# Layer order and rounding in a four-layer image kernel: the previous image's projection moved behind the next image's layer 1, scores set between its chunks, x transposed from the token tile, conv1's high part rounded by ScalarE

## The chip, the cores and the metric

The kernel runs on one core of a Trainium2 chip. The time is that of one launch on the device, in microseconds (us). Three runs of the kernel before gave 1370.06 us at the median, from 1369.67 to 1373.99. The engines are TensorE (PE in the profile, PEld its weight loads), VectorE (DVE), ScalarE (ACT), GpSimd (POOL) and SyncE (SP), which issues every DMA of this kernel.

## What is computed

The input x is 8 images of 64 x 64 pixels with 48 channels, float32. Four layers run one after the other on each image. Biases and norms are left out here; the kernel folds them into its weights.

```python
# L0: attention over the 4096 pixels n of an image, then three convolutions
q2 = l2n(q*q / sum_c(q*q), axis=channel);  k2 = l2n(k*k / sum_c(k*k), axis=pixel)
t2 = q2 @ (k2^T @ v) / sqrt(N);  attn = (v + t2) @ w_ln
y = leaky_relu(conv1x1(concat(attn, x), w1), 0.2)      # "conv1", 96 -> 96
y = leaky_relu(conv3x3(y, w2), 0.2)                    # "conv2", 96 -> 96
x = conv1x1(y, w3) + x                                 # "w3",    96 -> 48
# L1 and L3: relu, depthwise 3x3, pointwise 48 -> 48, norm
# L2: rw = sigmoid(mean(x) @ Wr) mixes 4 experts' weights for this image;
#     expand 48 -> 192, relu, depthwise 3x3, relu, project 192 -> 48, + x
```

## The kernel before, in words

**One loop over images, two images in it.** Each engine has its own hand-written instruction order. `iteration(f, attn, back)` works on three images: it runs conv2, w3, layer 1 and the routing and expansion of layer 2 for image `f`; the rest of layer 2 (depthwise taps, projection), layer 3 and the output of image `back` = f-1; and the attention and conv1 of image `attn` = f+1. Iterations 1 to 6 are a loop; iteration 0 has no `back`, iteration 7 no `attn`. A prologue does attention and conv1 of image 0, and an epilogue layers 2 and 3 of image 7. Engines meet only through semaphores.

**Chunks.** Conv1 and conv2 work in 8 chunks (512 pixels each, one PSUM bank), the layers on row pairs in 4. PSUM is four rings of two banks: a chunk may be written when the reader of the chunk two places before is done.

**Float32 as two parts.** The inputs of conv2, layer 1 and layer 3 are split into a rounded high part and a low part (the difference), and each convolution is three passes: high weights on high input, low weights on high input, high weights on low input. For conv1's output y1 and chunk k: ScalarE writes 0.2 times the bank into a buffer of `y1` (three buffers), VectorE takes the maximum with the bank (`L666`), VectorE rounds it into `y1_h` (`L668`), and GpSimd writes the low part `y1_l` (`L954`). `conv2` waits ahead of its first pass for all 8 high parts and ahead of its third for all 8 low parts.

**Pair convolutions (layers 1 and 3).** `pair_conv` needs neighbour rows in other partitions. `copy_beside` copies them from SBUF to SBUF with 7 DMAs for each half of the image (`L849`, `L853`). The first half can be copied when high and low parts of chunks 0 to 2 are there, the second when chunk 3 is. Chunks 0 and 1 of the convolution wait for the first half, chunks 2 and 3 for the second. Afterwards `copy_x2` (`L862`, 4 DMAs) copies layer 1's output for the expansion of layer 2.

**Layer 2 on VectorE.** The depthwise taps are 50 steps for an image on VectorE (`L623`, `L627`; the first tap of units 2 to 5 is ScalarE's). `steps_at` deals them out: 4 beside conv1, 40 beside conv2, 6 beside the projection. ScalarE's `finish_unit` does the relu of a finished unit, of which `project` chunk m needs numbers up to m + 2. `project` m writes a bank; ScalarE's `project_affine` turns it into layer 3's input `v` and its high part (`L1340`, `L1341`), and VectorE's `l3_low_part` makes the low part (`L704`). `project` m + 2 needs the high part of m.

**Order before, middle iterations.** TensorE: conv2 with w3(m) behind each odd pair, project 0, w3(3), project 1, layer 1 chunks 0 and 1, project 2 and 3, x transposes 0 and 1 (`L1006`), layer 1 chunk 2, transposes 2 and 3, layer 1 chunk 3, all scores (`L1018`), routing (`L1107`), layer 3 (4 chunks), attention sums (`L1030`), output transposes (`L1176`), attention weights, expansion and conv1 of the next image. SyncE: copies for layer 1, load of x in columns into the tile of the depthwise output (`load_xa`, 8 DMAs), copies for layer 3, load of x into the token tile (`load_x`, 8 DMAs), `copy_x2`, store.

## Time and profile before

| what | us |
|---|---|
| median of three runs | 1370.06 |
| profiled execution, its own time | 1369.96 |
| its span, from first to last instruction | 1368.2 |
| TensorE busy in it | 1211.5 (89%) |
| VectorE busy | 906.6 (66%) |
| ScalarE busy | 475.9 (35%) |
| GpSimd busy | 218.2 (16%) |

The span is 1.8 us short of the execution's own time. The six middle iterations repeat every 157.0 us to within a tenth, so one of them is read in detail: from the moment image 4's conv2 waits for its low parts to the same moment of image 5 (694.96 to 851.93). Idle time of TensorE is what to look for first, then what each engine was waiting for; a digit in the row PEclk of the page, or "PEclk" in a table of stretches, is the granted clock as a share of 2.4 GHz, and 0.50 is 1.2 GHz.

### The profile page before, as it was taken

To read this page: it belongs to the slowest core of one execution; us is meant where nothing else is said; L and a number is where in the kernel's file an instruction comes from. 1 tells how busy PE (TensorE), PEld (TensorE's weight loads), DVE (VectorE), ACT (ScalarE), POOL (GpSimd) and SP (SyncE) were. 2 spreads that over 40 slices of the span, in tenths; PEclk is the share of its full clock that TensorE was granted. 3 is DMA by queue.
4 is the path that set the end of the run, shared out by engine and by line. 5 is a ranking of instruction groups with operands and counts; after the bars stand their busy time and mean duration, and the time that the engine had idled before them with its cause. 6 is when DMAs were issued, how large, how long until landed. Compare 5 with 4: busy or idle time off the path is not lost.

```text
span 1368.2 us, 14700 instructions
## 1 busy us (share of the span) xinstructions
PE 1211.5 (89%) x4981; PEld 779.2 (57%) x4981; DVE 906.6 (66%) x1146; ACT 475.9 (35%) x812; POOL 218.2 (16%) x80
## 2 busy tenths in 40 slices
PE   3798788999789996999789996999879997999995
PEld 3565565657455674656556573656656574555543
DVE  5642477954978368964789358983789449884660
ACT  2211431335422542335512444235413354224331
POOL 0300034000610026000430007000340006000000
PEclk9699877999899997999989997999979998999998
DMA  3203700099003960079101980049300990039306
GB/s 59 42 14 43 105 0 0 1 127 123 23 0 39 135 97 0 0 93 135 43 0 25 121 126 0 0 66 139 66 0 0 128 120 23 0 40 127 60 11 91
DMA packets 200076, 76.06 MB, mean 56 GB/s; under 512 B 191245, under 2 KB 191858, under 8 KB 200050
## 3 DMA queue, kind: packets, MB, share of 16 engines
q1 hardware_dynamic: 200050, 75.73, 39.7%
q8 instruction: 15, 0.25, 0.1%
q14 instruction: 11, 0.09, 0.0%
HBM read 13.65 MB, written 6.29 MB: 15 GB/s over the span
## 4 chain that ended last, share of the span: by engine, by line
PE 50%; issue 18%; POOL 15%; SPq 7%; DVE 4%; DMA 3%; ACT 2%; POOLq 0%; DVEq 0%; ACTq 0%
PE bank L1074 29%; POOL y_parts L954 13%; PE bank L1098 4%; PE bank L1085 3%; SPq L828 3%; PE bank L1018 2%; SPq L853 2%; PE bank L1142 2%; PE bank L1165 2%; PE bank L1164 2%; POOL tok L949 2%; DMA y_parts<-a_parts 2%; PE bank L1101 1%; PE bank L1100 1%; SPq L849 1%
## 5 line engine op out<-in xcount | busy, mean ns | idle before, releaser
L1074 PE MATMUL bank<-y_parts,w_h 96*96 96x512 f32 x1152 | 329.9, 440 | 49.8 <-POOL y_parts L954 28.2
L1074 PEld LDWEIGHTS bank<-y_parts,w_h 96*96 96x96 f32 x1152 | 202.1, 177 | 162.8 <-POOL y_parts L954 31.6
L627 DVE SCALAR_TENSOR_TENSOR dwa<-h1a,dyn,dwa 128x1024 f32<-128x1024 f32 x240 | 294.1, 1273 | 0.0
L954 POOL TENSOR_TENSOR y_parts<-y,y_parts 96x512 fp32r<-96x512 f32 x64 | 194.8, 3044 | 211.7 <-DVE y_parts L668 211.7
L627 DVE SCALAR_TENSOR_TENSOR dwb<-h1b,dyn,dwb 128x1024 f32<-128x1024 f32 x128 | 155.8, 1273 | 0.0
L1074 PE MATMUL bank<-y_parts,w_l 96*96 96x512 f32 x576 | 153.9, 413 | 0.0
L949 POOL TENSOR_TENSOR tok<-tok,u 128x1536 f32<-128x1536 f32 x8 | 22.4, 2797 | 735.7 <-DVE u L568 735.7
L1098 PE MATMUL bank<-a_parts,wt_h 128*96 128x512 f32 x384 | 119.2, 419 | 15.9 <-DMA y_parts<-a_parts 15.9
L1074 PEld LDWEIGHTS bank<-y_parts,w_l 96*96 96x96 f32 x576 | 98.0, 170 | 47.5 <-issue 0.6
L1313 ACT ACTIVATE xq<-bank,b2s 96x512 f32<-96x512 f32 x32 | 21.9, 685 | 236.2 <-PE bank L1074 227.3
L704 DVE SCALAR_TENSOR_TENSOR a_parts<-v,a_parts 96x512 fp32r<-96x512 f32 x64 | 44.0, 687 | 85.8 <-ACT a_parts L1341 83.0
L1059 PE MATMUL bank<-xq,w_cur 97*96 97x512 f32 x128 | 70.0, 628 | 29.2 <-DVE y L666 28.5
L668 DVE CAST y_parts<-y 96x512 fp32r<-96x512 f32 x64 | 90.0, 1407 | 2.2
L1098 PEld LDWEIGHTS bank<-a_parts,wt_h 128*96 128x96 f32 x384 | 61.5, 165 | 46.8 <-issue 20.8
L1313 ACT ACTIVATE y<-bank,b2s 96x512 f32<-96x512 f32 x32 | 21.9, 684 | 144.1 <-PE bank L1074 144.1
L1030 PE MATMUL bank<-tok 128*97 128x48 f32 x512 | 55.0, 277 | 16.7 <-POOL tok L949 16.7
L681 DVE SCALAR_TENSOR_TENSOR xq<-bank,col,xq 96x512 f32<-96x512 f32 x32 | 23.8, 744 | 64.8 <-ACT xq L1313 64.8
L1164 PE MATMUL bank<-dwa,pc 128*96 128x512 f32 x128 | 65.4, 592 | 0.0
L1165 PE MATMUL bank<-dwb,pc 128*96 128x512 f32 x128 | 65.3, 592 | 0.0
L1030 PEld LDWEIGHTS bank<-tok 128*97 128x97 f32 x512 | 54.9, 195 | 17.9 <-issue 17.0
L717 DVE TENSOR_TENSOR y_parts<-y,y_parts 96x512 fp32r<-96x512 f32 x32 | 22.1, 689 | 60.6 <-ACT y_parts L1354 60.6
L1098 PE MATMUL bank<-a_parts,wt_l 128*96 128x512 f32 x192 | 57.4, 408 | 0.0
(222 smaller groups left out, 1700.1 us busy)
## 6 DMA issues: line engine op xcount, KB each, us to landing
y_parts<-a_parts SPq DMA_DIRECT2D x32, 396.0 KB, 6.1
y_parts<-a_parts SPq DMA_DIRECT2D x64, 192.0 KB, 6.6
a_parts<-a_parts SPq DMA_DIRECT2D x32, 264.0 KB, 3.3
dwa<-in_x_dram SPq DMA_DIRECT2D x64, 96.0 KB, 2.9
tok<-in_x_dram SPq DMA_DIRECT2D x64, 96.0 KB, 4.2
x_even<-y_parts SPq DMA_DIRECT2D x16, 384.0 KB, 8.8
x_odd<-y_parts SPq DMA_DIRECT2D x16, 384.0 KB, 8.6
out_dram<-dwb SPq DMA_DIRECT2D x32, 192.0 KB, 2.2
```

The lines of the kernel that those rows point to most:

```text
L627: nc.vector.scalar_tensor_tensor(out=dst, in0=tap_input(n, t), scalar=weight, in1=dst, op0=ALU.mult, op1=ALU.add).then_inc(tap_step, 1)
L668: nc.vector.tensor_copy(y1_view(y1_h, k - 1), y1_tokens(k - 1)).then_inc(y1h_ready, 1)
L704: return nc.vector.scalar_tensor_tensor(out=lo[:, rows, 1:W + 1], in0=src[:, m % 2, :].rearrange("p (j w) -> p j w", w=W), scalar=0.0, in1 ...
L949: nc.gpsimd.tensor_tensor(k, k, columns(u[:, :, :], 2 * RUN, [[1, 2 * RUN], [0, C]]), ALU.mult).then_inc(k_scaled, 1)
L954: nc.gpsimd.tensor_tensor(y1_view(y1_l, k), y1_tokens(k), y1_view(y1_h, k).bitcast(F32), ALU.subtract).then_inc(y1l_ready, 1)
L1030: last = nc.tensor.matmul(bank[0:SUMS, 0:C], token(par, i, X_AT, SUMS), token(par, i, K_AT, C), start=first, stop=final)
L1059: nc.tensor.matmul(bank[0:C2, :], w1_cur[:, :], xq[:, (k - 1) % 2, :], start=True, stop=True)\
L1074: last = nc.tensor.matmul(bank[0:C2, :], wgt[:, t, :], src[:, rows, cols], start=t + n == 0, stop=t == TAPS - 1 and n == 2)
L1098: nc.tensor.matmul(bank[0:C2, :], wgt[layer][:, kw, :], own[:, rows, kw:kw + W], start=n + kw == 0, stop=False)
L1164: nc.tensor.matmul(bank[0:C2, :], pc[:, 0, cols], first[:, :, par, :], start=False, stop=False)
L1165: last = nc.tensor.matmul(bank[0:C2, :], pc[:, 1 + m // 2, cols], other[:, :, par, :], start=False, stop=par == 1)
L1313: nc.scalar.activation(y2[(k // 2) % 2][:, (k % 2) * BANK:(k % 2 + 1) * BANK], ring_c.bank(C_2 + k)[0:C2, :], ACT.Identity, bias=b2s[:, 0: ...
```

## The change

Six things are changed.

1. **Projection.** `project`, `project_affine` and the copies for layer 3 of image `back` move from beside layer 1 of image `f` to behind it: project 0, routing, project 1 to 3, attention sums, layer 3 chunks 0 and 1, attention weights, chunks 2 and 3. On VectorE, `norms_begin` (the norms of the attention) now stands ahead of `route`, and `norms_end` between `l3_low_part` 1 and 2.
2. **Scores and transposes.** x transposes 0 and 1 come ahead of w3(3), 2 and 3 behind layer 1 chunk 0; scores 0 to 3 behind chunk 1 and 4 to 7 behind chunk 2.
3. **x from the token tile.** `load_xa` is gone. `load_x` is first in SyncE's iteration and has 12 DMAs: x, and the even rows once more beside the odd ones in the place of q, so that `transpose_x` reads pairs from the token tile.
4. **Conv1's rounding.** ScalarE copies the bank unscaled (`y1_linear`), VectorE forms max(0.2 y, y) from SBUF alone in one instruction, ScalarE rounds to the high part (`y1_high_part`), GpSimd writes the low parts of chunks 0 to 6 and VectorE that of chunk 7 (`y1l_last`).
5. **Conv2.** w3(m) goes behind the first pass of chunk 2m + 2, where it was behind all three; the wait for low parts stays ahead of the third pass of chunk 0.
6. **Taps.** 6 beside conv1, 4 beside each conv2 chunk, 12 beside layer 1. q's fourth powers go to `y1`, layer 1's output buffer to `xq`.

```diff
-        steps_at = (0, 1, 1, 1, 0, 1, 0, 0) + (8, 5, 5, 5, 5, 4, 4, 4) + (1, 1, 1, 3)
+        steps_at = (0, 1, 1, 1, 1, 1, 1, 0) + (4,) * CHUNKS + (1, 1, 2, 3, 3, 2)
-        expand_beside = {BEFORE: (0, 1), 0: (2,), 1: (3, 4), 7: (), 8: (10, 11), **{k: (k + 3,) for k in range(2, 7)}}
+        expand_beside = {BEFORE: (0, 1), 7: (), 8: (9, 10, 11), **{k: (k + 2,) for k in range(7)}}
 # VectorE, conv1_out
-                    dve.wait_ge(y1_slope, CHUNKS * image + k)
-                    bank = ring_c.bank(C_1 + k - 1)
-                    nc.vector.tensor_tensor(y1[:, buffer, :], bank[0:C2, :], y1[:, buffer, :], ALU.max).then_inc(y1_max, 1)
-                    dve.wait_ge(y1_max, CHUNKS * image + k)
-                    nc.vector.tensor_copy(y1_view(y1_h, k - 1), y1_tokens(k - 1)).then_inc(y1h_ready, 1)
+                    dve.wait_ge(y1_linear, CHUNKS * image + k)
+                    nc.vector.scalar_tensor_tensor(out=y1[0:C2, buffer, :], in0=y1[0:C2, buffer, :], scalar=SLOPE,
+                                                   in1=y1[0:C2, buffer, :], op0=ALU.mult, op1=ALU.max).then_inc(y1_max, 1)
+                if image is not None:
+                    dve.wait_ge(y1h_ready, CHUNKS * image + CHUNKS)
+                    nc.vector.tensor_tensor(y1_view(y1_l, CHUNKS - 1), y1_tokens(CHUNKS - 1),
+                                            y1_view(y1_h, CHUNKS - 1).bitcast(F32), ALU.subtract).then_inc(y1l_last, 1)
 # VectorE, iteration: behind the last x2_low_part
-                route(f)
-                if attn is not None:
-                    norms_begin(attn)
-                mix_weights(f)
-                if attn is not None:
-                    norms_end(attn)
+                depthwise_at(back, BY_L1 + 5)
+                if attn is not None:
+                    norms_begin(attn)
+                route(f)
+                for m in range(2) if back is not None else ():
+                    l3_low_part(back, m)
+                if attn is not None:
+                    norms_end(attn)
+                for m in range(2, PCHUNKS) if back is not None else ():
+                    l3_low_part(back, m)
+                mix_weights(f)
 # ScalarE, iteration: behind l1_out(f, (3,))
+                if attn is not None:
+                    fourth_powers(attn)
                 if back is not None:
                     project_affine(back, f + 1, 0)
                     finish_unit(back, 4)
                     finish_unit(back, 5)
                 route(f)
-                if attn is not None:
-                    fourth_powers(attn)
+                for m in range(1, PCHUNKS) if back is not None else ():
+                    project_affine(back, f + 1, m)
+                if attn is not None:
+                    root_of_q(attn)
                 if back is not None:
                     l3_out(back, (0, 1))
 # SyncE
             def iteration(f, attn, back):
+                if attn is not None:
+                    load_x(sp, attn)
                 beside_l1(sp, f)
-                if attn is not None and back is not None:
-                    load_xa(sp, attn, PCHUNKS * (f - 1) + 2)
                 if back is not None:
                     beside_l3(sp, back, f + 1)
-                if attn is not None:
-                    load_x(sp, attn)
                 copy_x2(sp, f)
 # GpSimd
-                for k in range(CHUNKS):
+                for k in range(POOL_CHUNKS):      # 7
```

**TensorE, from the end of layer 1 to layer 3 of a middle iteration.** Before (L1101 is layer 1 and 3, L1018 scores, L1107 routing, L1030 sums, L1176 output):

```order
L1101 MATMUL bank<-y_parts,wt_h 96x512
...
L1018 MATMUL bank<-qkw,xcm 128x192 x2
...
L1107 MATMUL bank<-wr,mean_b 128x4
...
L1098 MATMUL bank<-a_parts,wt_h 96x512 x3
...
L1030 MATMUL bank<-tok 97x48 x32
L1176 MATMUL bank<-ident,dwa 128x96 x16
```

Now (L1087 is layer 1, L1149 to L1151 the projection, L1093 routing, L1014 sums, L1084 layer 3):

```order
L1087 MATMUL bank<-y_parts,wt_h 96x512
...
L1149 MATMUL bank<-x_even,pick 96x512
L1150 MATMUL bank<-dwa,pc 96x512
L1151 MATMUL bank<-dwb,pc 96x512
...
L1093 MATMUL bank<-wr,mean_b 128x4
...
L1149 MATMUL bank<-x_even,pick 96x512
...
L1014 MATMUL bank<-tok 97x48 x32
...
L1084 MATMUL bank<-a_parts,wt_h 96x512 x3
```

Between the last chunk of layer 1 and the first of layer 3 stood the scores and the routing; now the four chunks of the projection stand there, then the sums.

**VectorE, the same place.** Before (L717 is `x2_low_part`, L729 `route`, L566 to L574 `norms_begin`, L741 the start of `mix_weights`, L581 and L584 `norms_end`):

```order
L717 TENSOR_TENSOR y_parts<-y,y_parts 96x8x64 [waits x2h_ready]
L729 TENSOR_TENSOR rwz<-bank,br 128x4 [waits rw_done]
...
L566 TENSOR_REDUCE s<-tok 128x64 [waits squared]
...
L574 TENSOR_SCALAR s<-s 128x64 [waits attn_chain]
L741 TENSOR_TENSOR prod<-lin,rw 128x92 [waits rw_ready]
...
L581 RECIPROCAL r<-s 128x32 [waits root_q]
...
L584 TENSOR_TENSOR tok<-tok,r 128x32x48 [waits attn2_chain]
```

Now (L629 a tap, L568 to L576 `norms_begin`, L731 `route`, L706 `l3_low_part`, L583 and L586 `norms_end`):

```order
L719 TENSOR_TENSOR y_parts<-xq,y_parts 96x8x64 [waits x2h_ready]
...
L629 SCALAR_TENSOR_TENSOR dwa<-h1a,dyn,dwa 128x1024 [waits tap_step]
...
L568 TENSOR_REDUCE s<-tok 128x64 [waits squared]
...
L731 TENSOR_TENSOR rwz<-bank,br 128x4 [waits rw_done]
L706 SCALAR_TENSOR_TENSOR a_parts<-v,a_parts 96x8x64 [waits ah3_ready,v3_ready] x2
L583 RECIPROCAL r<-s 128x32 [waits root_q]
...
L586 TENSOR_TENSOR tok<-tok,r 128x32x48 [waits attn2_chain]
L706 SCALAR_TENSOR_TENSOR a_parts<-v,a_parts 96x8x64 [waits ah3_ready,v3_ready] x2
L743 TENSOR_TENSOR prod<-lin,rw 128x92 [waits rw_ready]
```

`norms_begin` passed ahead of `route`, and the low parts of layer 3's chunks 2 and 3 stand behind the whole of the norms.

**ScalarE, the same place**, now (L1256 fourth powers, L1344 and L1345 `project_affine`, L1363 `route`, L1260 `root_of_q`); before, all of `project_affine` stood ahead of the end of layer 1:

```order
L1256 ACTIVATE y<-tok 128x1536 [waits squared]
...
L1344 ACTIVATE v<-bank,dyn 96x512 [waits al1_ready]
L1345 ACTIVATE a_parts<-bank,dyn 96x8x64
...
L1363 ACT_TABLE_LOAD
L1363 ACTIVATE rw<-rwz 128x4 [waits rwz_ready]
...
L1344 ACTIVATE v<-bank,dyn 96x512 [waits al1_ready,project_done]
...
L1344 ACTIVATE v<-bank,dyn 96x512 [waits al3_ready,project_done]
...
L1260 ACT_TABLE_LOAD
L1260 ACTIVATE s<-s 128x32 [waits norm_q]
```

`project_affine` 1 to 3 stand behind `route`, and `root_of_q` behind them.

## Rows read from the trace of the kernel before

**Rows 1.** The page: busy us of each engine (share of the span), instructions.
```profile
PE 1211.5 (89%) x4981; PEld 779.2 (57%) x4981; DVE 906.6 (66%) x1146; ACT 475.9 (35%) x812; POOL 218.2 (16%) x80
```

**Rows 2.** Table of stretches, one middle iteration: length, each engine's busy us, clock, DMA.
```profile
core 0: us, PE busy (x) PEld busy (x) DVE busy (x) ACT busy (x) POOL busy (x), PEclk, DMA share, GB/s
694.96:749.50 54.54, 54.54 (x211) 35.45 (x212) 48.07 (x45) 12.88 (x16) 0.00 (x0) 0.96 0.04 7
749.50:784.30 34.80, 33.45 (x122) 18.44 (x121) 14.46 (x17) 14.91 (x25) 0.00 (x0) 1.00 1.02 128
784.30:813.50 29.20, 28.32 (x179) 22.54 (x177) 15.88 (x34) 14.81 (x32) 2.80 (x1) 1.00 0.96 127
813.50:851.93 38.43, 27.36 (x106) 16.66 (x103) 33.45 (x37) 16.64 (x28) 25.91 (x8) 0.84 0.05 20
```

**Rows 3.** Timeline of TensorE, conv2 starts: start us, us, instructions [idle before <-releaser].
```profile
683.85 4.16 PE L1074 MATMUL bank<-y_parts,w_h 96*96 96x512 f32 x9 [3.17 <-DVE y_parts L668]
...
694.96 6.55 PE L1074 MATMUL bank<-y_parts,w_h 96*96 96x512 f32 x18 [4.18 <-POOL y_parts L954]
...
703.49 4.47 PE L1074 MATMUL bank<-y_parts,w_h 96*96 96x512 f32 x18
```

**Rows 4.** Timeline of GpSimd, low parts of y1, chunks 6 and 7.
```profile
838.61 1.69 POOL L954 TENSOR_TENSOR y_parts<-y,y_parts 96x512 fp32r<-96x512 f32 x1 [0.55 <-DVE y_parts L668]
840.85 11.03 POOL L954 TENSOR_TENSOR y_parts<-y,y_parts 96x512 fp32r<-96x512 f32 x1 [0.55 <-DVE y_parts L668]
```

**Rows 5.** Timeline of VectorE beside them: maximum, rounding, eight taps.
```profile
838.46 0.67 DVE L666 TENSOR_TENSOR y<-bank,y 96x512 f32<-96x512 f32 x1
839.17 1.60 DVE L668 CAST y_parts<-y 96x512 fp32r<-96x512 f32 x1
840.69 9.64 DVE L627 SCALAR_TENSOR_TENSOR dwb<-h1b,dyn,dwb 128x1024 f32<-128x1024 f32 x8
```

**Rows 6.** Timeline of TensorE from projection 1 to the output transposes.
```profile
754.59 0.79 PE L1163 MATMUL bank<-x_even,pick 96*96 96x512 f32 x1
...
758.49 1.28 PE L1098 MATMUL bank<-a_parts,wt_h 128*96 128x512 f32 x3
...
784.23 1.46 PE L1018 MATMUL bank<-qkw,xcm 97*128 97x192 f32 x8
...
791.11 0.93 PE L1098 MATMUL bank<-a_parts,wt_h 128*96 128x512 f32 x3
...
805.45 5.61 PE L1030 MATMUL bank<-tok 128*97 128x48 f32 x64
810.89 2.35 PE L1176 MATMUL bank<-ident,dwa 96*128 96x96 f32 x16
```

**Rows 7.** Timeline of VectorE: last low part of layer 1's output, norms.
```profile
785.99 0.69 DVE L717 TENSOR_TENSOR y_parts<-y,y_parts 96x512 fp32r<-96x512 f32 x1 [0.20 <-ACT y_parts L1354]
...
791.76 3.35 DVE L566 TENSOR_REDUCE s<-tok 128x64 f32<-128x3072 f32 x1 [0.30 <-ACT tok L1260]
...
799.11 0.18 DVE L574 TENSOR_SCALAR s<-s 128x32 f32<-128x32 f32 x1
...
805.13 1.76 DVE L584 TENSOR_TENSOR tok<-tok,r 128x1536 f32<-128x1536 f32 x1
```

**Rows 8.** Timeline of ScalarE: the second half of project_affine 0, a table load.
```profile
754.16 0.68 ACT L1341 ACTIVATE a_parts<-bank,dyn 96x512 fp32r<-96x512 f32 x1
...
791.74 1.28 ACT L1359 ACT_TABLE_LOAD   x1
```

**Rows 9.** Timeline of SyncE: first DMA of layer 3's first-half copies, iteration 4.
```profile
773.82 0.65 SPq L849 DMA_DIRECT2D a_parts<-a_parts  x1
```

**Rows 10.** Epilogue: SyncE issues the same copies, TensorE waits; a stretch of the DMA.
```profile
1330.91 0.65 SPq L849 DMA_DIRECT2D a_parts<-a_parts  x1
...
1342.81 1.57 PE L1098 MATMUL bank<-a_parts,wt_h 128*96 128x512 f32 x3 [10.17 <-DMA y_parts<-a_parts]
...
1350.00:1352.00 2.00, 2.00 (x10) 1.39 (x9) 0.00 (x0) 0.00 (x0) 0.00 (x0) 1.00 0.36 32
```

More of the change, by code:

```diff
@@ L819, in x_rows @@
             return a["x"][image].rearrange("(j b) (q i) c -> b q j i c", b=2, q=WQ)
-        def load_xa(sp, image, projected):
-            src = x_rows(image)
-            wait(sp, project_done, projected)
-            by_column = xa.rearrange("p (i b c) -> p b i c", b=2, c=C)
-            for n in range(2 * WQ):
-                par, q = n % 2, n // 2
-                sp.dma_start(by_column[q::WQ, par], src[par, q]).then_inc(xa_loaded, 16)
         def load_x(sp, image):
@@ L836, in load_x @@
                 sp.dma_start(tok[q::WQ, par, :, X_AT:X_AT + C], src[par, q]).then_inc(x_loaded, 16)
+            for q in range(WQ):
+                sp.dma_start(tok[q::WQ, 1, :, Q_AT:Q_AT + C], src[0, q]).then_inc(x_loaded, 16)
         def copy_beside(sp, n, half):
@@ L1180, in l1, with l3, prepare_norms @@
                 pair_conv(image, L1, ring_b, B_L1, l1_done, chunks)
-            def l3(image):
-                pair_conv(image, L3, ring_d, D_L3, l3_done, range(PCHUNKS))
+            def l3(image, chunks):
+                pair_conv(image, L3, ring_d, D_L3, l3_done, chunks)
+            def prepare_norms():
+                pe.wait_ge(prep_dve, marks["pairs"])
+                pe.wait_ge(wt_placed, 16 * WT_COPIES)
+                nc.tensor.matmul(banks[7][:, 128:128 + C], ones[0:C, :], norm3[:, :], start=True, stop=True).then_inc(prep_pe, 1)
+                for n in range(2):
+                    rows, cols = slice(0, (M1, M2)[n]), slice(n * M1, (M1, M)[n])
+                    nc.tensor.matmul(banks[7][0:C2, 192 + cols.start:192 + cols.stop], ones[rows, 0:C2], norm1[rows, cols],
+                                     start=True, stop=True).then_inc(prep_pe, 1)
@@ L1187, in iteration @@
+                if attn is not None:
+                    attention_scores(attn, range(4, 8))
+                l1(f, (3,))
                 if back is not None:
                     project(back, (0,))
-                w3(f, PCHUNKS - 1)
-                if back is not None:
-                    project(back, (1,))
-                else:
-                    pe.wait_ge(prep_dve, marks["pairs"])
-                    pe.wait_ge(wt_placed, 16 * WT_COPIES)
-                    nc.tensor.matmul(banks[7][:, 128:128 + C], ones[0:C, :], norm3[:, :], start=True, stop=True).then_inc(prep_pe, 1)
-                    for n in range(2):
-                        rows, cols = slice(0, (M1, M2)[n]), slice(n * M1, (M1, M)[n])
-                        nc.tensor.matmul(banks[7][0:C2, 192 + cols.start:192 + cols.stop], ones[rows, 0:C2], norm1[rows, cols],
-                                         start=True, stop=True).then_inc(prep_pe, 1)
@@ L1251, in x_out, with scores_out @@
                         .then_inc(xcm_ready, 1)
-            def scores_out(image):
-                for n in range(8):
+            def scores_out(image, banks_of_two):
+                for n in banks_of_two:
                     act.wait_ge(qk_done, 8 * image + n + 1)
@@ L1409, in iteration @@
                 if back is not None:
-                    l3_out(back, (0, 1))
+                    project_affine(back, f + 1, 0)
+                    finish_unit(back, 4)
+                    finish_unit(back, 5)
+                route(f)
+                for m in range(1, PCHUNKS) if back is not None else ():
+                    project_affine(back, f + 1, m)
                 if attn is not None:
```

178 lines of the change are left out of this document (87 added, 91 removed).

## The prediction

> **What bounds the kernel now.** I read the page's busy shares first: TensorE is busy 89% of the span, no other engine over 66% [rows 1]. So the question is where TensorE idles and whether the change fills those holes or makes new ones. The table of stretches answers it for one middle iteration of 157.0 us [rows 2]: TensorE idles 0.0, 1.3 and 0.9 us in the first three stretches and 11.1 us in the last, conv1 of the next image and the start of conv2. There the clock is 0.84 on average; elsewhere it is full or nearly. The timeline shows the end of that stretch: conv2 waits 3.2 us for VectorE's last high part, and behind 18 matmuls 4.2 us for GpSimd's last low part [rows 3]. A second reading of rows 2 matters more here: from 749.5 to 813.5 the DMA share is 1.02 and 0.96, the copies run all through layers 1 and 3, and yet TensorE hardly waits for them. Layer 3's first copies are issued at 773.82 [rows 9], and layer 3 starts at 791.11 [rows 6], 17.3 us later; the projection was done early enough. That cover is what the change takes away.
>
> **Conv1 and the start of conv2.** GpSimd and VectorE exclude each other here: the last low part takes 11.03 us where the one before takes 1.69 [rows 4], because eight taps of 9.64 us run from 840.69 [rows 5] and it finishes about 1.6 us after them. The rounding of 1.60 us ends 0.5 us after the low part beside it, but the maximum of 0.67 us, with one input in PSUM, costs GpSimd nothing [rows 4, 5]. The change makes chunk 7's low part VectorE's and ahead of the taps, so the 4.2 us wait goes. What is late next is the chain of exclusive work before it. Before: 7 low parts of 1.69 (11.8 us), 8 roundings of about 0.6 (5), 4 taps (4). Now: 7 low parts (11.8), 8 maxima that read SBUF twice, of 0.65 (5.2), 6 taps (6.4), and one more turn to ScalarE and back. ScalarE has four instructions a chunk of 0.59 on average (16.64 us for 28 in that stretch [rows 2]), 2.4 us, beside it. I take conv2 starting 1 us later than now; at best the rest of the stretch's idle time goes (11.1 - 4.2 = 6.9 us), at worst it starts 5 us later, if each turn to ScalarE costs 0.6 us. Conv2's start now also loses about 5 us at half clock: 9 matmuls take 4.16, later 18 take 4.47 [rows 3]. Without the second stop I estimate 4 lost. Sum: -4.2 + 1 - 1 = -4.2 us.
>
> [...]
>
> **From conv2's end to layer 1's end.** This takes 34.9 us now (749.4 to 784.2), with the projection's 4 x 3.9 us in it (754.59 to 758.49 is one) [rows 6]. Now the scores (6.9 us, 784.23 to 791.11) take its place. w3 comes 18 matmuls (4.4 us [rows 3]) earlier: w3(2) ends 45 matmuls, 10.7 us, ahead of conv2's end. The sum with the shortcut, the high part, two taps and the low part take about 4.4 (1.1, 0.6, 2.4, 0.7; estimates but for the taps), and the first half of the copies is issued at -6.1. How long a half takes stands in the epilogue: 1330.91 to 1342.81, 11.9 us [rows 10]. Layer 1 could start at +3.3 (my estimate: the last y2 on two engines 1.5, w3 1.7) and starts at +5.8. Its four chunks take 3.6 us each (791.11 to 805.45 is four) [rows 6]. Adding transposes (0.9), two groups of scores (3.8 each) and a low clock at its start (1), layer 1 ends at +29.7. The second half, issued at +6.6, lands at +18.5, when TensorE gets there. Sum: 29.7 - 34.9 = -5.2 us. Between -8 and 0, by the wait for the copies. The x loads go to conv2, where the DMA share is 0.04 [rows 2]: they cost nothing, and the 1.3 us of idle in the second stretch, the transposes' wait for them, goes.
>
> **From layer 1's end (t = 0, now 784.23) to the expansion (now 813.5, +29.3).** Step by step:
> - VectorE ends layer 1's last low part at +2.4 (785.99 + 0.69) [rows 7], two taps of 1.2 at +4.8, `norms_begin` (791.76 to 799.29, 7.5 us) at +12.3. Only then `route`, +12.5. The routing's wait thus has the norms queued ahead of it.
> - ScalarE finishes project_affine 0 and two units at +7.4, loads its table (1.28) [rows 8] and stands at `route` until +12.7. project_affine 1 is two instructions of 0.68, +14.0.
> - TensorE runs projection 0 to 2 by +11.9; number 3 needs the high part of 1 and runs from +14.1 to +18.0. Idle 2.2.
> - project_affine 3 at +19.4; table load and root at +20.9; `norms_end` (the 1.76 of rows 7 and two short ones, 2.3) at +23.3; only then VectorE's low part 2 at +24.0. SyncE issues layer 3's first half at +24.3. It lands 11.9 later, **+36.2**.
> - TensorE ends the sums (5.4) [rows 6] at +23.5 and idles **12.7 us**. After such a stop layer 3's first chunk ran 6.0 us in the epilogue (from 1342.81, at 0.50 clock), so chunks 0 and 1 end at +45.8. Both halves land 19.7 us after the first issue (in 1350 to 1352 the share falls to 0.36) [rows 10], +44.0: no further wait.
> - Chunks 2 and 3 with the weights 7.6, outputs 2.35 behind a wait of 1: **+56.7**. `copy_x2` is behind these copies on SyncE and lands near +55.3 to +59: about level.
> Sum: 56.7 - 29.3 = +27.4 us. Least +22 (no low clock, a shorter norm chain), most +31.
>
> **The sum.** A middle iteration: -4.2 - 5.2 + 27.4 = +18.0, six times +108. The last iteration has no norms; its low part 2 comes at about +14, its half at +26 against sums that do not exist: about 10.4 idle, 2.4 at low clock, and the layer 1 wait, +17. Iteration 0 has no projection: conv1 -4, and copies and scores moved ahead about -3, -7. The prologue loads 12 where 8 DMAs came before the first transposes (+2.5) and has one low part less (-2). Total +118 or +119 on the execution's 1369.96 (span 1368.2, 0.1 below the median): **1489 us**.
>
> **The rivals.**
> A. Conv1 is no longer held by the exclusive pair: the new maximum or ScalarE's share lets conv1 run at TensorE's own pace, 5 to 8 us less per image, seven times: 1489 - 45 = 1444. For: VectorE loses eight roundings of up to 1.60. Against: two SBUF inputs, as the taps have, and two taps more. Chance 0.09.
> B. The turn VectorE, ScalarE, GpSimd with three buffers sets the pace: +4 us per image, or copy_x2 lands at +59: 1489 + 31 = 1520. For: ScalarE must now answer twice per chunk. Chance 0.17.
> C. The other side: layer 3 does not wait for its copies. Place: between the sums and layer 3. If the first half lands by +23.5, where the sums end, the 12.7 idle and 2.4 of low clock go, and with the 2.2 ahead of projection 3 the iteration is 157.7, within a us of now; the last one is +5, iteration 0 -7: 1372, and with A's gain 1330. It decides at the issue: SyncE would have to start at +11.6 and not at +24.3. For: now it starts 17 us ahead. Against: three waits in a row (route behind the norms, projection 3, norms_end) stand before it. Chance 0.05, half of it faster, and 0.01 of it slower.
> D. The chain is shorter than I add it up, because ScalarE or VectorE gets ahead: half of the 12.7 us is there, 1489 - 45: again 1444. Chance 0.09.
>
> **How the numbers follow.** The forecast has 0.60, A and D 0.18, B 0.17, C 0.05. The range holds all but C and the ends of A and B: 1438 to 1530. A measurement of this kernel can tell about 0.3% (4 us) from no change. Slower: 0.96; same: 0.015; faster: 0.025.
>
> **What would show it.** TensorE's longest wait of a middle iteration should be ahead of layer 3's chunk 0, released by a DMA into y_parts, 10 to 14 us, with the clock at 0.50 behind it; a second one of 2 to 3 us ahead of layer 1. The period should be about 175 us. GpSimd's 11 us low part should be gone, and with it the 4.2 us of rows 3. DMA share should be near zero in the 20 us ahead of layer 3's copies. I am wrong if layer 3's copies are issued less than 18 us after layer 1's end, or if the last stretch of rows 2, from the expansion to conv2's third pass (38.4 us), comes out below 32 or over 39.

## The result, and the profile after

The changed kernel took 1492.6, 1489.15 and 1486.73 us, the kernel before 1370.27 us at the median of four runs beside them: a ratio of 1.0864, 95% interval 1.0828 to 1.09. A fourth run of the changed kernel fell in a slow state (2025.76 us at a clock of 0.55) and is compared with nothing. The prediction was 1489 us. Below, a difference from the changed kernel is counted from 1489.15 us, the median of the three. The profiled execution took 1492.6 us, with a span of 1490.8.

The page of the changed kernel, busy us of each engine (compare [rows 1]):

```profile
PE 1241.5 (83%) x4981; PEld 789.0 (53%) x4981; DVE 871.8 (58%) x1090; ACT 531.8 (36%) x876; POOL 170.3 (11%) x72
```

TensorE has the same 4981 matmuls and is busy 30.0 us longer, at a lower mean clock (0.903, before 0.928); the other 92.6 us of the 122.6 that the span grew are idle time. The table of stretches of image 4's iteration has the boundaries of [rows 2]: conv2's third pass, its end, the end of layer 1, the expansion, the next third pass. The columns are length, busy us of TensorE, its weight loads, VectorE, ScalarE and GpSimd, clock, DMA share and GB/s:

```profile
747.76:800.05 52.29, 52.29 (x212) 33.91 (x211) 43.87 (x41) 12.78 (x16) 0.00 (x0) 1.00 0.09 16
800.05:829.46 29.41, 24.11 (x113) 17.11 (x112) 16.46 (x17) 11.69 (x31) 0.00 (x0) 1.00 0.56 62
829.46:887.07 57.61, 42.76 (x187) 25.89 (x186) 21.18 (x43) 16.97 (x26) 2.79 (x1) 0.85 0.64 74
887.07:921.42 34.35, 27.50 (x104) 16.52 (x104) 26.03 (x25) 24.60 (x36) 19.01 (x7) 0.90 0.24 57
```

Against [rows 2] the four are -2.2, -5.4, **+28.4** and -4.1 us. Three stretches gained, and the third lost more than twice what they gained. The middle iterations are not all alike: from third pass to third pass they take 173.1 to 177.0 us, 174.6 on average, and those of the kernel before 157.0 to 157.7 us, 157.3 on average (not 157.0 to within a tenth). TensorE's timeline shows its waits there (start, us, instructions, idle before and releaser). Layer 1's end is 829.46, where projection 0 starts:

```profile
843.37 0.46 PE L1149 MATMUL bank<-x_even,pick 96*96 96x512 f32 x1 [1.84 <-ACT a_parts L1345]
...
845.32 1.42 PE L1149 MATMUL bank<-x_odd,pick 96*96 96x512 f32 x1
...
849.02 5.61 PE L1014 MATMUL bank<-tok 128*97 128x48 f32 x64
...
866.55 1.60 PE L1084 MATMUL bank<-a_parts,wt_h 128*96 128x512 f32 x3 [11.91 <-DMA y_parts<-a_parts]
...
884.92 2.37 PE L1162 MATMUL bank<-ident,dwa 96*128 96x96 f32 x16 [0.96 <-ACT dwa L1368]
```

The 11.91 us are the longest wait of the iteration. What held the copies stands in VectorE's timeline:

```profile
834.23 3.34 DVE L568 TENSOR_REDUCE s<-tok 128x64 f32<-128x3072 f32 x1
...
841.66 0.15 DVE L731 TENSOR_TENSOR rwz<-bank,br 128x4 f32<-128x4 f32 x1
841.73 0.68 DVE L706 SCALAR_TENSOR_TENSOR a_parts<-v,a_parts 96x512 fp32r<-96x512 f32 x1
843.35 0.69 DVE L706 SCALAR_TENSOR_TENSOR a_parts<-v,a_parts 96x512 fp32r<-96x512 f32 x1 [0.94 <-ACT a_parts L1345]
852.05 0.35 DVE L583 RECIPROCAL r<-s 128x32 f32<-128x32 f32 x1 [8.01 <-ACT s L1260]
...
854.34 1.29 DVE L706 SCALAR_TENSOR_TENSOR a_parts<-v,a_parts 96x512 fp32r<-96x512 f32 x2
```

`route` (L731) stands behind 7.4 us of `norms_begin`. VectorE then idles 8.01 us for ScalarE's root with the low parts of chunks 2 and 3 queued behind that wait, though the high part of chunk 2 had been there since 844.4. SyncE's timeline has the issue right behind the first of them, and the table of stretches shows the 20 us ahead of it, the wait, and layer 3's first chunk:

```profile
855.13 0.59 SPq L841 DMA_DIRECT2D a_parts<-a_parts  x1
```

```profile
835.10:855.10 20.00, 17.69 (x91) 10.11 (x89) 10.71 (x15) 8.30 (x12) 2.79 (x1) 0.91 0.00 0
854.64:866.55 11.91, 0.00 (x1) 0.01 (x1) 6.01 (x22) 0.00 (x0) 0.00 (x0) 0.65 1.03 137
866.55:872.60 6.05, 6.05 (x16) 4.03 (x17) 0.00 (x0) 0.00 (x0) 0.00 (x0) 0.55 1.20 139
```

For 20 us no DMA runs while TensorE works, then for 11.9 us TensorE stands while all DMA engines work. Of the two stops of [rows 3] at conv2's start, the 4.18 us are gone and the 3.17 us are 0.78; ahead of the last chunk of conv1 stands a stop of 3.29 us, before 2.33:

```profile
909.40 1.94 PE L1043 MATMUL bank<-xq,w_cur 97*96 97x512 f32 x2 [3.29 <-ACT xq L1275]
...
915.54 3.56 PE L1060 MATMUL bank<-y_parts,w_h 96*96 96x512 f32 x9 [0.78 <-ACT y_parts L1296]
918.90 2.68 PE L1060 MATMUL bank<-y_parts,w_l 96*96 96x512 f32 x9
921.42 4.43 PE L1060 MATMUL bank<-y_parts,w_h 96*96 96x512 f32 x18
```

In conv1 the long low part of [rows 4] is gone, and GpSimd's rows read like this (all 56 of them took 2649 ns on average, before 3044):

```profile
898.81 17.09 POOL L939 TENSOR_TENSOR y_parts<-y,y_parts 96x512 fp32r<-96x512 f32 x6 [0.59 <-ACT y_parts L1296]
```

### The profile page after: what moved, and what is told of

Its sections match the earlier page's. It is cut to its first block, busy times and chain, and to the rows that moved or that the text cites. A ratio compares the mean times of both kernels' runs of the same rounds, so it can differ in the third digit from the quotient of the medians.

```text
span 1490.8 us, 14638 instructions
## 1 busy us (share of the span) xinstructions
PE 1241.5 (83%) x4981; PEld 789.0 (53%) x4981; DVE 871.8 (58%) x1090; ACT 531.8 (36%) x876; POOL 170.3 (11%) x72
## 4 chain that ended last, share of the span: by engine, by line
PE 44%; issue 32%; POOL 8%; DMA 5%; SPq 5%; ACT 3%; DVE 3%; POOLq 0%; ACTq 0%; DVEq 0%
PE bank L1060 29%; POOL y_parts L939 6%; DMA y_parts<-a_parts 5%; PE bank L1071 4%; PE bank L1084 3%; SPq L845 2%; PE bank L1128 2%; SPq L841 2%; POOL tok L934 1%; PE bank L1003 1%; DVE y L667 1%; PE bank L1086 1%; PE bank L1087 1%; ACT y_parts L1296 1%; PE bank L1014 1%
## 5 line engine op out<-in xcount | busy, mean ns | idle before, releaser
L1060 PE MATMUL bank<-y_parts,w_h 96*96 96x512 f32 x1152 | 300.0, 414 | 2.8 <-ACT y_parts L1296 2.8
L629 DVE SCALAR_TENSOR_TENSOR dwa<-h1a,dyn,dwa 128x1024 f32<-128x1024 f32 x240 | 294.2, 1274 | 0.0
L1060 PEld LDWEIGHTS bank<-y_parts,w_h 96*96 96x96 f32 x1152 | 192.8, 168 | 98.2 <-ACT y_parts L1296 6.4
L1084 PE MATMUL bank<-a_parts,wt_h 128*96 128x512 f32 x384 | 126.0, 440 | 118.8 <-DMA y_parts<-a_parts 118.7
L939 POOL TENSOR_TENSOR y_parts<-y,y_parts 96x512 fp32r<-96x512 f32 x56 | 147.1, 2649 | 376.5 <-ACT y_parts L1296 376.1
L1060 PE MATMUL bank<-y_parts,w_l 96*96 96x512 f32 x576 | 162.4, 427 | 0.0
L629 DVE SCALAR_TENSOR_TENSOR dwb<-h1b,dyn,dwb 128x1024 f32<-128x1024 f32 x128 | 157.4, 1274 | 0.0
L1084 PEld LDWEIGHTS bank<-a_parts,wt_h 128*96 128x96 f32 x384 | 64.6, 177 | 155.8 <-DMA y_parts<-a_parts 89.2
L667 DVE SCALAR_TENSOR_TENSOR y<-y 96x512 f32<-96x512 f32 x64 | 85.8, 1341 | 34.1 <-ACT y L1282 33.4
L1368 ACT ACTIVATE dwa<-bank,conv_bias,inv 96x512 f32<-96x512 f32 x32 | 24.8, 774 | 224.0 <-PE bank L1087 224.0
L1319 ACT ACTIVATE xq<-bank,b2s 96x512 f32<-96x512 f32 x32 | 21.9, 685 | 159.3 <-PE bank L1060 150.4
L1296 ACT ACTIVATE y_parts<-y 96x512 fp32r<-96x512 f32 x64 | 72.7, 1135 | 3.8 <-DVE y L667 3.8
L1151 PE MATMUL bank<-dwb,pc 128*96 128x512 f32 x128 | 68.4, 618 | 0.0
L1014 PE MATMUL bank<-tok 128*97 128x48 f32 x512 | 55.0, 277 | 15.4 <-POOL tok L934 15.4
L1333 ACT ACTIVATE a_parts<-v 96x512 fp32r<-96x512 f32 x32 | 20.4, 636 | 129.9 <-DVE v L695 129.9
L1014 PEld LDWEIGHTS bank<-tok 128*97 128x97 f32 x512 | 55.0, 195 | 18.9 <-issue 18.9
L1084 PE MATMUL bank<-a_parts,wt_l 128*96 128x512 f32 x192 | 63.7, 445 | 0.0
L1354 ACT ACTIVATE xq<-bank,conv_bias,inv 96x512 f32<-96x512 f32 x32 | 24.8, 774 | 108.1 <-PE bank L1087 108.1
```

Source lines behind the costliest of these rows:

```text
L629: nc.vector.scalar_tensor_tensor(out=dst, in0=tap_input(n, t), scalar=weight, in1=dst, op0=ALU.mult, op1=ALU.add).then_inc(tap_step, 1)
L667: nc.vector.scalar_tensor_tensor(out=y1[0:C2, buffer, :], in0=y1[0:C2, buffer, :], scalar=SLOPE, in1=y1[0:C2, buffer, :], op0=ALU.mult, op ...
L939: nc.gpsimd.tensor_tensor(y1_view(y1_l, k), y1_tokens(k), y1_view(y1_h, k).bitcast(F32), ALU.subtract).then_inc(y1l_ready, 1)
L1014: last = nc.tensor.matmul(bank[0:SUMS, 0:C], token(par, i, X_AT, SUMS), token(par, i, K_AT, C), start=first, stop=final)
L1060: last = nc.tensor.matmul(bank[0:C2, :], wgt[:, t, :], src[:, rows, cols], start=t + n == 0, stop=t == TAPS - 1 and n == 2)
L1084: nc.tensor.matmul(bank[0:C2, :], wgt[layer][:, kw, :], own[:, rows, kw:kw + W], start=n + kw == 0, stop=False)
```

## The experiments

Two questions were open: whether the loss is really the chain in front of the copies and their length (a1 to a5), and what the gain in conv1 is made of (b1, b2, c1, d1, e1, f1). b3 and d1 put the gains together. Times without a range (a1, a2, a4, a5, e1, c1) are single executions; the three of the changed kernel spread over 6 us, so a difference of a few microseconds in them says little. The kernel before took 1370.4 to 1371.6 us at the median beside the runs.

### Order on VectorE: the routing ahead of the norms

```diff
+                route(f)
                 if attn is not None:
                     norms_begin(attn)
-                route(f)
```

> The changed kernel with VectorE's routing step ahead of norms_begin; nothing else is touched. Theory 1 (the chain route, affine, norms_end, low part 2, issue sets layer 3's wait): ScalarE no longer stands until +12.4, projection 3's wait of 1.8 us goes, and SyncE issues layer 3's first half at about +21.5 after layer 1's end instead of +25.7; the wait ahead of layer 3 shrinks by about as much less the 1.8 us, the iteration by 4.4 us, six times 26: about 1464. Rival (the low parts of chunks 2 and 3 behind norms_end hold it alone, the routing has slack): 1485 to 1491.

Measured: 1466.2 us, 23 less than the changed kernel. The size came out, the place only in part. TensorE's and SyncE's timelines of this kernel, layer 1 ends at 814.39:

```profile
830.20 5.61 PE L1014 MATMUL bank<-tok 128*97 128x48 f32 x64
...
847.83 1.59 PE L1084 MATMUL bank<-a_parts,wt_h 128*96 128x512 f32 x3 [12.02 <-DMA y_parts<-a_parts]
```

```profile
836.31 0.59 SPq L841 DMA_DIRECT2D a_parts<-a_parts  x1
```

The issue is at +21.9 instead of +25.7, but the wait ahead of layer 3 has its full 12.02 us. Projection 3 no longer waits and runs at full clock, so the sums also start 3.8 us earlier (+15.8, not +19.6), and both ends of the wait moved together. A wait's length does not tell what an edit won; the position of its end does.

### Order on VectorE: the low parts ahead of norms_end

```diff
-                for m in range(2) if back is not None else ():
+                for m in range(PCHUNKS) if back is not None else ():
                     l3_low_part(back, m)
                 if attn is not None:
                     norms_end(attn)
-                for m in range(2, PCHUNKS) if back is not None else ():
-                    l3_low_part(back, m)
```

> The changed kernel with VectorE's l3_low_part 2 and 3 ahead of norms_end; nothing else is touched. Theory 1: low part 2 comes at about +16.6 instead of +25.0, the issue at about +17, the half lands at about +28.5; layer 3's wait of 11.9 us falls to about 3.5 us, the iteration by 8.7 us and perhaps 1 more by the clock, six times 52 to 58: 1432 to 1439. Rival (the order of VectorE is not what holds it; the next wait in the row, ScalarE's affine 2 and 3 or the transfer itself, comes as late): 1480 to 1491.

Measured: 1434.9 us, 54 less. From the timelines:

```profile
816.56 0.58 SPq L839 DMA_DIRECT2D a_parts<-a_parts  x1
```

```profile
828.22 0.96 PE L1082 MATMUL bank<-a_parts,wt_h 128*96 128x512 f32 x3 [2.31 <-DMA y_parts<-a_parts]
```

The half lands 11.7 us behind its issue (11.4 in the changed kernel), and the wait is 2.31 us. The first rows of layer 3 run at full speed (0.96 us for three matmuls, 1.60 behind the long stop), but the clock falls behind them, as the table of stretches shows (clock 0.94 in the first 1.28 us, 0.51 in the next 3.30):

```profile
828.22:829.50 1.28, 1.28 (x5) 0.91 (x6) 1.11 (x6) 0.00 (x0) 0.00 (x0) 0.94 1.25 201
829.50:832.80 3.30, 3.30 (x9) 2.17 (x8) 1.65 (x8) 0.00 (x0) 0.00 (x0) 0.51 1.10 128
```

Two calls in another order are worth 54 us of 119.

### Both orders

> Both: routing ahead of norms_begin, and low parts 2 and 3 ahead of norms_end. Theory 1: issue at about +16, landing at +27.5, projection 3 without its 1.8 us wait, the sums end near +23; wait ahead of layer 3 about 4 to 5 us; the iteration 9.7 to 11 us shorter: 1424 to 1432, and so still over 50 us above the kernel before, because the copies' 11.5 us have only the sums' 5.5 us as cover. Rival (order alone explains the loss): within 10 us of the kernel before, 1360 to 1380.

Measured: 1426.6 us (1425.3 to 1429.2), ratio to the kernel before 1.0407, interval 1.0382 to 1.0432. Layer 3's chain in this kernel; layer 1 ends at 794.47:

```profile
809.67 0.59 SPq L839 DMA_DIRECT2D a_parts<-a_parts  x1
```

```profile
810.27 5.61 PE L1012 MATMUL bank<-tok 128*97 128x48 f32 x64
821.28 1.59 PE L1082 MATMUL bank<-a_parts,wt_h 128*96 128x512 f32 x3 [5.40 <-DMA y_parts<-a_parts]
```

Issue at +15.2, landing at +26.8, 11.6 us later. The rival, that the order explains all, falls: 55 us of loss remain with the best order of these two steps.

### One copy of seven

Of layer 3's copies of each half only the one into its own tile is kept; the other six are left out, so layer 3 reads layer 1's neighbour rows (in this run and in a5).

```diff
                 sp.dma_start(to, frm).then_inc(b_copied[n][half], 16)
+                if n == L3:
+                    return
```

> The changed kernel with one of layer 3's seven copies of each half (the one into its own tile); the six others are left out, so layer 3 reads neighbour rows that are layer 1's. Theory 1 (the wait is the issue at +25.7 plus the length of the copies): the issue stays at +25.7, the half lands 3 to 5 us later instead of 11.4, the wait ahead of layer 3 is 3.5 to 5.5 us instead of 11.9; seven iterations and the epilogue's layer 3: 1423 to 1443. Rival (something else, ScalarE or VectorE, is equally late): the wait stays above 9 us and the time above 1470.

Measured: 1416.5 us, 73 less than the changed kernel, 6.5 us below the range. In the traces the six middle iterations are 50 us shorter, and what follows them (the last iteration and the epilogue) 25. The wait of image 4's iteration:

```profile
827.70 1.60 PE L1086 MATMUL bank<-a_parts,wt_h 128*96 128x512 f32 x3 [3.57 <-DMA a_parts<-a_parts]
```

The copy lands 3.1 us behind its issue (824.63) and the wait is 3.57 us, not 11.91. So the wait is issue time plus copy length, and nothing else that layer 3 waits for is as late.

### Both orders and one copy

> The changed kernel with routing and low parts ahead of the norms, and one of layer 3's seven copies of each half (the six others are left out, so layer 3 reads layer 1's neighbour rows). Theory (what is left of the loss after the reordering is the copies' length, for which only the sums stand as cover): the wait of 5.4 us ahead of layer 3 goes and its first chunk runs at full clock, about 7.4 us per middle iteration and about 17 in the last one and the epilogue: 1358 to 1380. Rival (the wait goes but another takes its place ahead of layer 3): above 1395.

Measured: 1373.8 us, with no wait ahead of layer 3 in the middle iterations: its first row stands right behind the sums, at full clock.

```profile
793.99 5.61 PE L1014 MATMUL bank<-tok 128*97 128x48 f32 x64
799.43 0.94 PE L1084 MATMUL bank<-a_parts,wt_h 128*96 128x512 f32 x3
```

The order takes away 62.5 us and the copies' length 53 more. But only 31 of these 53 lie in the six middle iterations. The other 22 lie in the last iteration and the epilogue, and in the epilogue the kernel before waits for the same copies too (10.17 us, [rows 10]), so the 53 are not all a loss that the change made.

### Conv1 alone on the kernel before

Part 4 of the change, with the old table of taps.

> The kernel before with part 4 of the change alone: ScalarE copies the bank and rounds, VectorE takes the maximum from SBUF, GpSimd has 7 low parts and VectorE the last, expand_beside as in the changed kernel, four taps beside conv1 as before. Theory (the prediction's term, with the size that the changed kernel's trace gave it): the 4.2 us stop at conv2's third pass and about 2 us of low clock behind it go, seven times: 1326 to 1342. Rival (conv1 gains only when the projection is elsewhere, since GpSimd and ScalarE are more loaded here): 1355 to 1372.

Measured: 1320.2 us (1318.0 to 1323.4), ratio 0.9634, interval 0.9602 to 0.9665: 50 us less than the kernel before, and below the range. A middle iteration is 7.3 us shorter, where 6.2 were expected; what the seventh microsecond is made of no run shows.

### One low part moved

```diff
+                if image is not None:
+                    dve.wait_ge(y1h_ready, CHUNKS * image + CHUNKS)
+                    nc.vector.tensor_tensor(y1_view(y1_l, CHUNKS - 1), y1_tokens(CHUNKS - 1),
+                                            y1_view(y1_h, CHUNKS - 1).bitcast(F32), ALU.subtract).then_inc(y1l_last, 1)
-                for k in range(CHUNKS):
+                for k in range(POOL_CHUNKS):      # 7, GpSimd
```

> The kernel before with one edit: VectorE, not GpSimd, makes the low part of conv1's chunk 7, right behind its high part and ahead of the taps. Theory 1 (the stop is one low part starved by eight taps): it gives the whole of part 4's gain or nearly, 1328 to 1345. Rival (part 4's gain comes from ScalarE's share, the rounding that it took from VectorE): 1355 to 1370.

Measured: 1325.9 us (1323.2 to 1328.9), ratio 0.9675, interval 0.9641 to 0.9709. One instruction that changes its engine is worth 44 us, most of b1's 50. VectorE's timeline shows why: it takes 1.10 us here, where GpSimd needed 11.03 beside the same eight taps.

```profile
663.86 1.10 DVE L673 TENSOR_TENSOR y_parts<-y,y_parts 96x512 fp32r<-96x512 f32 x1
664.88 9.65 DVE L629 SCALAR_TENSOR_TENSOR dwb<-h1b,dyn,dwb 128x1024 f32<-128x1024 f32 x8
```

### The table of taps alone

```diff
-        steps_at = (0, 1, 1, 1, 0, 1, 0, 0) + (8, 5, 5, 5, 5, 4, 4, 4) + (1, 1, 1, 3)
+        steps_at = (0, 1, 1, 1, 0, 1, 0, 0) + (4, 6, 6, 6, 5, 5, 4, 4) + (1, 1, 1, 3)
```

> The kernel before with one line changed: the table of taps has 4 steps, not 8, beside conv2's chunk 0, and one or two more beside each of chunks 1 to 5. Nothing of conv1 is touched. Theory 1 (the stop needs the long row of eight taps behind the last high part): GpSimd's last low part takes about 6.3 us instead of 11.0, it ends before conv2's third pass, the stop of 4.2 us and about 2 us of low clock go, seven times: 1322 to 1335. Rival (the taps moved later are missed by the projection or by the routing, or the stop stays): 1345 to 1372.

Measured: 1333.1 us (1329.7 to 1337.6), ratio 0.9715, interval 0.9689 to 0.9741. GpSimd still has the last low part, with four taps beside it instead of eight, and conv2's third pass starts as it ends (669.81 + 6.30 = 676.11), with no stop of more than 0.15 us in any iteration:

```profile
669.81 6.30 POOL L954 TENSOR_TENSOR y_parts<-y,y_parts 96x512 fp32r<-96x512 f32 x1 [0.54 <-DVE y_parts L668]
```

```profile
676.16 4.53 PE L1074 MATMUL bank<-y_parts,w_h 96*96 96x512 f32 x18
```

### The old conv1 in the changed kernel

Part 4 undone: VectorE takes the maximum with the bank and rounds, GpSimd has 8 low parts. The new table, with 4 taps beside conv2's chunk 0, stays.

> The changed kernel with the old conv1 (part 4 undone: VectorE takes the maximum with the bank and rounds, GpSimd has all 8 low parts); the new table of taps stays, 6 beside conv1 and 4 beside conv2's chunk 0. Theory 1 (the stop at conv2's third pass hangs on the eight taps that stood behind the last high part): with four taps there the last low part ends in time, no stop, but two more taps beside conv1 on a loaded VectorE start conv2 1.5 to 3 us later: 1498 to 1515. Rival (the old conv1 brings its 4.2 us stop and the low clock along wherever it stands): 1520 to 1545.

Measured: 1497.6 us, 8 more than the changed kernel (half a microsecond outside the range) and little beyond the spread of its runs; a middle iteration is 1.6 us longer on average. So in the changed kernel the new conv1 brings only about 8 us: with the new table and the old conv1 TensorE waits 0.25 us at most ahead of conv2's third pass. The stop ahead of the first pass is back (3.21 us). GpSimd's last low part is again 6.28 us:

```profile
917.74 6.28 POOL L937 TENSOR_TENSOR y_parts<-y,y_parts 96x512 fp32r<-96x512 f32 x1 [0.54 <-DVE y_parts L670]
```

### The maximum's input in PSUM

```diff
-        ring_c = Ring(banks[4:6], [(y1_linear, CHUNKS, n + 1) for n in range(CHUNKS)]
+        ring_c = Ring(banks[4:6], [(y1_max, CHUNKS, n + 1) for n in range(CHUNKS)]
-                    nc.vector.scalar_tensor_tensor(out=y1[0:C2, buffer, :], in0=y1[0:C2, buffer, :], scalar=SLOPE,
+                    nc.vector.scalar_tensor_tensor(out=y1[0:C2, buffer, :], in0=ring_c.bank(C_1 + k - 1)[0:C2, :], scalar=SLOPE,
```

> The changed kernel with one operand changed: the new maximum reads its first input from the PSUM bank, not from SBUF, as the old one did; the bank comes free with the maximum. Theory 1 (two SBUF inputs exclude GpSimd): GpSimd's low parts fall from 2.65 us on average to 1.7, the maxima from 1.34 to 0.7, ScalarE's wait of 1.75 us for GpSimd ahead of the last chunk goes, conv1 is 1.5 to 3.5 us shorter, seven times: 1466 to 1481. Rival (GpSimd is slow by itself or the turn by ScalarE paces conv1): low parts as now and 1487 to 1494.

Measured: 1471.9 us, 17 less than the changed kernel; a middle iteration is 2.4 us shorter. The groups of maxima, low parts and ScalarE's copies of the bank (count, busy us in all, mean ns, idle before) of this kernel:

```profile
L939 POOL TENSOR_TENSOR y_parts<-y,y_parts 96x512 fp32r<-96x512 f32 x56 | 120.6, 2163 | 382.2 <-ACT y_parts L1296 381.2
L667 DVE SCALAR_TENSOR_TENSOR y<-bank,y 96x512 f32<-96x512 f32 x64 | 43.8, 685 | 43.7 <-ACT y L1282 43.7
L1282 ACT ACTIVATE y<-bank 96x512 f32<-96x512 f32 x64 | 38.7, 605 | 7.6 <-PE bank L1043 6.2 <-POOL y_parts L939 1.4
```

and of the changed kernel:

```profile
L939 POOL TENSOR_TENSOR y_parts<-y,y_parts 96x512 fp32r<-96x512 f32 x56 | 147.1, 2649 | 376.5 <-ACT y_parts L1296 376.1
L667 DVE SCALAR_TENSOR_TENSOR y<-y 96x512 f32<-96x512 f32 x64 | 85.8, 1341 | 34.1 <-ACT y L1282 33.4
L1282 ACT ACTIVATE y<-bank 96x512 f32<-96x512 f32 x64 | 38.2, 596 | 23.9 <-POOL y_parts L939 18.7 <-PE bank L1043 5.2
```

One operand moved halves the maxima (1341 to 685 ns) and shortens the low parts from 2649 to 2163 ns, though the instruction does the same arithmetic on as many elements. The low parts did not fall to the 1.7 us expected, and the taps beside them still have two SBUF inputs: beside no tap they take 1.71 us, beside one 2.40 to 2.74. ScalarE's 18.7 us of waiting for GpSimd fall to 1.4, and the stop of 3.29 us ahead of conv1's last chunk to 1.45. So in the changed kernel the pair of VectorE and GpSimd held the end of conv1; the run shortens the maxima and the low parts at once and does not tell their shares. This is the rule that the Trainium skill gives ("SBUF — State Buffer", section "Who interferes with whom": a VectorE instruction with two SBUF inputs contends with a GpSimd one that reads SBUF, and one with at most one input does not, unless it runs in one of VectorE's two-port modes, which a cast can enter). The trace agrees for the taps and both maxima. It does not agree for the old rounding, a cast with one SBUF input, unless that ran in such a mode, which no trace here shows: GpSimd held it as well (numbers in the last section).

### The gains put together

The kernel before with parts 3, 4 and 5 (x from the token tile, conv1, w3 behind the first pass); projection, scores, norms and taps as they were.

> The kernel before with parts 3, 4 and 5 of the change: conv1's rounding, x transposed from the token tile, w3 behind the first pass; projection, scores, taps and norms stay where they were. Theory (the loss is the projection's move alone): the transposes' wait of 1.3 us and up to 0.9 us around w3(3) go as well, 1315 to 1335. Rival (the twelve loads or the earlier w3 cost something that the changed kernel hides): above the run with part 4 alone by 5 us or more.

Measured: 1316.2 us (1315.3 to 1317.2), ratio 0.9597, interval 0.9568 to 0.9627. Parts 3 and 5 add 4 us to b1's 50, where 1.3 + 0.9 us per image would have been 13; the two intervals overlap, so even the 4 are not certain. The run also sizes the loss without the gains: with these gains and without the moved projection the time is 1316, so the move and what goes with it (parts 1, 2 and 6) cost 173 us, not 119. No run tells these three parts from each other.

The same with the maximum's first input in PSUM:

> The kernel before with parts 3, 4 and 5, and in it the maximum's first input in PSUM instead of SBUF (the bank comes free with the maximum). Theory 1 (here ScalarE's five instructions a chunk, 2.57 us, pace conv1, and GpSimd keeps up either way): low parts and maxima get shorter, the time stays, 1311 to 1318. Rival (the exclusive pair still holds conv1's end, as in the changed kernel): 1300 to 1309.

Measured: **1312.6 us** (1312.2 to 1315.2), ratio 0.9584, interval 0.9568 to 0.9600, the fastest kernel of this study. As expected the low parts got shorter (1907 ns, in b3 2296) and the time moved little (3.6 us, the intervals overlap). Here ScalarE paces conv1, with a copy to `xq`, a copy of the bank, the rounding and a relu for each chunk, one after the other without a gap:

```profile
793.93 0.62 ACT L1272 ACTIVATE xq<-bank 96x512 f32<-96x512 f32 x1
794.40 0.64 ACT L1279 ACTIVATE y<-bank 96x512 f32<-96x512 f32 x1
794.88 1.19 ACT L1293 ACTIVATE y_parts<-y 96x512 fp32r<-96x512 f32 x1
795.93 0.73 ACT L1380 ACTIVATE h1a<-bank,dyn 128x512 f32<-128x512 f32 x1
796.51 0.63 ACT L1272 ACTIVATE xq<-bank 96x512 f32<-96x512 f32 x1
```

One turn takes 2.58 us, from 793.93 to 796.51.

## Why the prediction was right, point by point

**The moved projection.** The chain was worked out step by step from layer 1's end. Predicted and measured: last low part +2.4, +2.5; `norms_begin` done +12.3, +12.3; `route` +12.5, +12.4; projection 3 starts +14.1, +13.9; it ends +18.0, **+19.6**; `norms_end` done +23.3, +25.0; issue +24.3, +25.7; landing +36.2, +37.1; expansion +56.7, +57.6. The one step that failed by over a microsecond is projection 3: I gave it TensorE's full clock, and behind its stop of 1.84 us it ran part of the way at half (0.70 on average from 843.37 to 849.02; a matmul row of 0.79 us reads 1.42). In the last two middle iterations of the same trace the clock stays full behind the same stop (1.00), and the number I gave is right there. The other steps carry that error along, and the copies' length, taken as 11.9 from [rows 10], gave back half a microsecond (11.4). +28.4 where +27.4 was predicted. That this chain is the cause, and not only that its end came out, is shown by a1, a2, a3 and a5.

**From conv2's end to layer 1's end.** -5.4 against -5.2. The first half of the copies was issued at -6.1, as predicted, though my four terms add up to 4.8 and not to 4.4 and would have given -5.9; the second at +6.9 (+6.6), and layer 1 started at +5.4 (+5.8), behind a wait of 1.7 us where I expected 2 to 3.

**Conv1 and conv2's start.** Right in sign, too small: -4.1 in the fourth stretch and -2.2 in the first, -6.3 together, against -4.2. Conv2 starts 28.5 us after the expansion, 1.2 later than before (1 predicted), and the stop of 4.2 is gone; so the full clock gave back about 3 us, where I had counted 1. That the start itself came out was luck, since the terms of its chain were far too small: the seven low parts took 14.9 us before (25.91 less 11.03 in [rows 2] and [rows 4]) and 19.0 now, not 11.8, the eight roundings about 11, not 5, and the eight maxima take 10.7, not 5.2. The mechanism was half right. The exclusive pair does hold conv1 (c1), and a low part of chunk 7 on VectorE does remove the stop (b2). But the stop had two sufficient cures in this change: f1 and e1 show that four taps instead of eight beside conv2's chunk 0, as in the new table, remove it alone. I credited the edit that I could name and did not ask what the other did to the same wait. On the sum this had no effect; as advice for the next edit it would have.

**The sum.** Counted from third pass to third pass, as the prediction counts, the span grew by 2.0 us up to image 0's (predicted 0.5), shrank by 3.4 in iteration 0 (predicted 7), and grew by 103.6 in the six middle iterations (944.0 to 1047.6, predicted 108) and by 20.4 in the last iteration and the epilogue (201.8 to 222.3, predicted 17). In the last iteration TensorE waits 6.2 and 10.0 us for the copies, where I had 10.4 us and a wait of 2 to 3 ahead of layer 1. In iteration 0 the stop went (3.5 us there), as predicted, and the 3 us for copies and scores did not. Earlier scores bring nothing there, since the sums wait for GpSimd's scaled k in either kernel (7.7 us before, 7.5 now), and from the sums to conv2's start it is 2.0 us longer than before. In the prologue the transposes did wait 2.5 us longer for the twelve loads, but no 2 us came back: conv2 waits for a column made by VectorE's preparation (5.64 us, before 4.90), not for a low part. These misses are 8.5 us too low together, and the six iterations 4.4 too high. That the median of three is met to within a microsecond is luck: the sum is 4 us below the profiled execution.

**The rivals.** A (conv1 no longer held by the pair) did not happen; c1 shows what one operand in PSUM brings towards it, 17 us of A's 45. B's mechanism, ScalarE's turn as the pace, is second in line: it appears in b3 and d1, where GpSimd keeps up. C (layer 3 does not wait) named the condition rightly, and a5 meets it from two sides, an earlier issue and a shorter copy: 1373.8 us, where C said 1372. That the numbers are so close is in part chance. The middle iterations are 158.8 us on average, where C said 157.7, and a5 leaves out copies in the last iteration and the epilogue too, which are 4.3 us shorter than before, where C had 5 more. D did not happen.

**What stays open.** a5 and b3 are still 58 us apart. The timelines show where TensorE stands in one and not in the other: two waits of 1.7 and 1.3 us ahead of layer 1's chunks 0 and 2 for its copies, 0.8 ahead of w3(3), two of the scores' waits of 0.75 instead of one, 1.0 ahead of the output, and 3.3 us instead of 1.5 before the last conv1 chunk: about 7 us in all per iteration. One wait of 1.0 us, early in conv2, stands in b3 alone. In the iteration read TensorE idles 12.6 us in a5 and 6.4 in b3, and is busy 146.6 and 142.5 us, at a clock of 0.94 and 0.97: 6.2 and 4.1 us; the six middle iterations differ by 60 us, and the rest of a5 is 2 us shorter. Each of these was read, not tested by a run.

## What to carry to other kernels

Before moving a producer of a copy closer to its reader, write down when the copy will be issued, how long it takes and what work stands between: here 11.5 us of copies had 17 us of cover and were left with the 5.6 us of the sums. In an in-order engine, a wait for a slow engine (the root, the routing) belongs behind everything that others already wait for; two such calls in the wrong order cost 62.5 us. And when a short instruction on GpSimd is slow, look at what VectorE runs beside it before giving it to another engine: fewer taps behind it (38 us), or the instruction on VectorE (44 us), were worth nearly as much as the whole rewrite of conv1 (50 us).
